# Experts of a pair interleaved over the partitions, one gate transfer a pair, and the routing bias moved to VectorE

## The reference

```
xn = layernorm(x)
# scan, per batch, feature d and state n of 16
dt = clamp(softplus(xn @ Wdt.T + bdt));  dA = exp(clamp(dt * A));  h = dA * h + dt * B * xn
y  = sum_n h * C + Dp * xn               # h is rescaled where its norm passes 20
# experts: 64 of them, hidden width 64, 8 chosen per token out of 4 of 8 groups
scores = sigmoid(xn @ router.T);  sfc = scores + correction_bias
groups: sum of the 2 best sfc of each group of 8, best 4 groups kept
chosen: best 8 of the kept sfc;  c = 2.5 * scores / sum(scores) for the chosen, else 0
routed = sum_e c_e * (relu(xn @ up_e)^2 @ down_e);  shared = relu(xn @ sup)^2 @ sdown
out = x + y + routed + shared
```

## Time and profile before

| | us |
|---|---|
| median of 3 runs | 610.81 |
| the runs | 602.62, 610.81, 615.13 |
| the profiled execution | 602.45 |
| its span, from the first to the last instruction | 600.7 |
| DVE (VectorE) busy in it | 498.6 |
| PE (TensorE) busy in it | 518.7 |

### The profile page before, as it was taken

One profiled execution on the slowest core, in us unless ns is written; L12 is line 12 of the kernel. 1 busy time (PEld: TensorE's weight loads), 2 busy tenths in 40 slices (PEclk: granted clock), 3 DMA queues, 4 the chain that ended last, 5 costly groups with the idle time before them and its releaser, 6 DMA issues. The chain is left out here.

```text
span 600.7 us, 8042 instructions
## 1 busy us (share of the span) xinstructions
PE 518.7 (86%) x1666; PEld 279.2 (46%) x1666; DVE 498.6 (83%) x1158; ACT 469.5 (78%) x922; POOL 468.8 (78%) x430
## 2 busy tenths in 40 slices
PE   2169889989899889998898988999899988998895
PEld 1036345545455444564454535555355544553442
DVE  3658898879988799887988799889999889886774
ACT  2758898778887798796986988888988887885662
POOL 2499798777989689786989879897899769765554
PEclk9999999997999999998999999999999999999999
DMA  9969998999999998999999999899999999899991
GB/s 203 301 176 254 257 242 232 224 249 259 251 265 260 251 279 258 244 243 251 241 279 262 272 286 254 251 268 288 272 283 244 251 263 262 237 236 243 256 250 48
DMA packets 67634, 149.34 MB, mean 249 GB/s; under 512 B 16032, under 2 KB 33024, under 8 KB 67584
## 3 DMA queue, kind: packets, MB, share of 16 engines
q1 hardware_dynamic: 65712, 147.07, 96.6%
q10 hardware_dynamic: 1872, 1.75, 1.1%
HBM read 143.03 MB, written 5.77 MB: 248 GB/s over the span
## 5 line engine op out<-in xcount | busy, mean ns | idle before, releaser
L1083 PE MATMUL DN<-act,down 128*128 128x512 f32 x512 | 264.4, 599 | 1.4 <-ACT act L710 1.3
L532 POOL TENSOR_TENSOR bc_rows<-dtx_all,bc_rows 128x512 f32<-128x512 f32 x128 | 164.1, 1283 | 87.0 <-DMA bc_rows<-bc_dram 86.8
L710 ACT ACTIVATE act<-relu 128x512 f32<-128x512 f32 x272 | 169.3, 623 | 69.7 <-DVE relu L880 63.9
L880 DVE SCALAR_TENSOR_TENSOR relu<-U,gate_rows 128x512 f32<-128x512 f32 x256 | 173.5, 678 | 42.7 <-DMA gate_rows<-gate_dram 19.2
L1033 PE MATMUL U<-x_hi,up_hi 128*128 128x512 f32 x256 | 159.0, 621 | 42.5 <-DVE relu L880 41.0
L541 POOL TENSOR_TENSOR yacc<-yacc,bc_rows 128x512 f32<-128x512 f32 x120 | 154.1, 1284 | 7.4 <-DVE bc_rows L892 7.1
L939 DVE TENSOR_TENSOR_SCAN DC<-DC,carry,bc_rows 128x512 f32<-128x512 f32 x96 | 122.7, 1278 | 0.0
L1033 PEld LDWEIGHTS U<-x_hi,up_hi 128*128 128x128 f32 x256 | 48.5, 189 | 144.7 <-DVE relu L880 105.6
L1083 PEld LDWEIGHTS DN<-act,down 128*128 128x128 f32 x512 | 96.3, 190 | 28.4 <-ACT act L710 5.6
L1035 PE MATMUL U<-x_hi,up_lo 128*128 128x512 f32 x256 | 102.0, 399 | 0.0
L1034 PE MATMUL U<-x_lo,up_hi 128*128 128x512 f32 x256 | 101.9, 398 | 0.0
(11 more groups left out here) (113 smaller groups left out, 503.8 us busy)
## 6 DMA issues: line engine op xcount, KB each, us to landing
bc_rows<-bc_dram SPq DMA_DIRECT2D x128, 512.0 KB, 10.7
gate_rows<-gate_dram SPq DMA_DIRECT2D x256, 256.0 KB, 8.7
xs<-in_L_attn_x SPq DMA_DIRECT2D x8, 256.0 KB, 5.7
down<-in_L_ffn_down_w SPq DMA_DIRECT2D x4, 512.0 KB, 7.3
xr<-in_L_attn_x SPq DMA_DIRECT2D x8, 256.0 KB, 11.5
rest_kept_dram<-rest SPq DMA_DIRECT2D x8, 256.0 KB, 9.1
out<-res SPq DMA_DIRECT2D x8, 256.0 KB, 7.7
dtx_all<-in_L_ffn_up_w SPq DMA_DIRECT2D x3, 512.0 KB, 6.6
```

What stands on the lines that cost most here:

```text
L532: g.tensor_tensor(b, dtx_all[:, sl(c)], b, ALU.mult).then_inc(dbp_done, 1)
L710: a.activation(act_at(c, slot), relu[:, slot % 2, :], ACT.Square).then_inc(sq_done, 1)
L880: v.scalar_tensor_tensor(out=relu[:, slot % 2, :], in0=U[slot % 2][:, :], scalar=0.0, in1=gate_rows[:, k // 2 % SBUFS, slot % 2, :], op0=A ...
L1083: mm(DN[:, :], w, act_at(c, slot), start=slot == 0, stop=slot == SLOTS - 1).then_inc(down_done, 1)
```

## The change

Three things change. First, the hidden units of a pair's two experts alternate over the partitions: unit i of the first expert lies on partition 2i, of the second on 2i + 1. The up weights are permuted when they are split into high and low part (read with a stride of 64 elements, in pairs), down is loaded by two DMAs a quarter, each to every second partition, and the gates of two pairs come in one transfer of 512 KB to 128 partitions, in which neighbouring partitions read from two different rows of DRAM. VectorE waits for one transfer instead of two. Second, the bias is added to the scores by VectorE, in slot 11.5, and not by GpSimd in slot 12; the wait of VectorE on GpSimd between them is gone, and so are two semaphores. Third, the routing behind it moves one slot up: VectorE's part from the group maxima to the sum of weights (slots 13 to 22.5 become 12 to 21.5), and GpSimd's L452 (slot 17 to 16) and L456, L459 (slot 18 to 17). ScalarE's slots, the later GpSimd steps and TensorE's transposes stay.

```diff
+        def side_by_side(t):
+            return t.rearrange("p (j e i) -> p j i e", e=2, i=I)
+        def paired(t):
+            return t.rearrange("p (j i e) -> p j i e", e=2, i=I)
...
-                sp.dma_start(down[:, e0 // 2:e1 // 2, :],
-                             down_in[e0:e1].rearrange("(j e) i h -> (e i) j h", e=2)).then_inc(w_down[q], 16)
+                for e in range(2):
+                    sp.dma_start(down[e:P:2, e0 // 2:e1 // 2, :],
+                                 down_in[e0:e1].rearrange("(j e) i h -> e i j h", e=2)[e]).then_inc(w_down[q], 16)
...
-                for half in range(2):
-                    for r in range(GCOPIES):
-                        part = slice(half * I + r * I // GCOPIES, half * I + (r + 1) * I // GCOPIES)
-                        row = half * PAIRS + 2 * i
-                        sp.dma_start(gate_rows[part, j, :, :],
-                                     gate_rows_of(c)[r:r + 1, row:row + 2].broadcast_to([I // GCOPIES, 2, CT])
-                                     ).then_inc(g_loaded[j], 16)
+                both = gate_rows_of(c)[0].rearrange("(e s) t -> e s t", e=2)[:, 2 * i:2 * i + 2, :]
+                sp.dma_start(gate_rows[:, j, :, :], both.unsqueeze(0).broadcast_to([I, 2, 2, CT])
+                             ).then_inc(g_loaded[j], 16)
...
-                if slot == 17:
+                if slot == 16:
                     pool.wait_ge(zpos_ready, pc + 1)
                     pool.wait_ge(log_done, pc + 1)
                     g.tensor_tensor(poly[:, :], poly[:, :], zpos[:, :], ALU.add).then_inc(sp_ready, 1)
-                if slot == 18:
+                if slot == 17:
                     pool.wait_ge(groups_ready, pc + 1)
...
-                if slot == 12:
-                    pool.wait_ge(sig_ready, pc + 1)
-                    alone(pool)
-                    g.tensor_tensor(sfc[:, :, :], sig[:, :, :], cbias[:, :].unsqueeze(1).broadcast_to([P, KB, E]),
-                                    ALU.add).then_inc(sfc_ready, 1)
...
-                g.tensor_tensor(up_lo[:, cols], up_raw[q], up_hi[:, cols].bitcast(F32),
+                g.tensor_tensor(paired(up_lo[:, cols]), side_by_side(up_raw[q]), paired(up_hi[:, cols].bitcast(F32)),
                                 ALU.subtract).then_inc(up_split, 1)
...
-                if slot == 12:
+                if slot == 25:
                     pool.wait_ge(w_late, 5 * 16)
...
-                a.activation(up_hi[:, cols], up_raw[q], ACT.Copy).then_inc(up_high, 1)
+                a.activation(paired(up_hi[:, cols]), side_by_side(up_raw[q]), ACT.Copy).then_inc(up_high, 1)
...
+                if slot == 11.5:
+                    if pc == 0:
+                        dve.wait_ge(w_late, 5 * 16)
+                    op(v.tensor_tensor, sfc[:, :, :], sig[:, :, :], cbias[:, :].unsqueeze(1).broadcast_to([P, KB, E]), ALU.add)
-                if slot in (13, 13.5, 14, 14.5):
-                    k = int(2 * (slot - 13))
+                if slot in (12, 12.5, 13, 13.5):
+                    k = int(2 * (slot - 12))
                     if k == 0:
-                        dve.wait_ge(sfc_ready, pc + 1)
+                        ch.wait(True)
...
-                if slot == 17.5:
+                if slot == 16.5:
                     ch.wait()
                     v.tensor_tensor(g1c[:, :], g1a[:, :], g1b[:, :], ALU.not_equal).then_inc(groups_ready, 1)
-                if slot in (19.5, 20):
-                    if slot == 19.5:
+                if slot in (18.5, 19):
+                    if slot == 18.5:
                         dve.wait_ge(masked_ready, pc + 1)
...
-                    dve.wait_ge(g_loaded[k // 2 % SBUFS], 32 * (k // 2 // SBUFS + 1))
+                    dve.wait_ge(g_loaded[k // 2 % SBUFS], 16 * (k // 2 // SBUFS + 1))
```

More of the change, by code:

```diff
@@ L201, in layer_program @@
         log_done = sem("log_done")
-        sig_one, sig_ready, sfc_ready = sem("sig_one"), sem("sig_ready"), sem("sfc_ready")
+        sig_one = sem("sig_one")
         cc_ready, ct_done, gate_ready, gate_stored = sem("cc_ready"), sem("ct_done"), sem("gate_ready"), sem("gate_stored")
@@ L256, in layer_program @@
         LEAD = 2
-        DVE_PREP = 11
+        DVE_PREP = 13
         POOL_PREP = 6
@@ L783, in constants @@
                     split = slice(0, E * I // QUARTERS)
-                    v.tensor_tensor(up_lo[:, split], up_raw[0], up_hi[:, split].bitcast(F32),
+                    v.tensor_tensor(paired(up_lo[:, split]), side_by_side(up_raw[0]), paired(up_hi[:, split].bitcast(F32)),
                                     ALU.subtract).then_inc(up_split, 1)
@@ L819, in prep @@
                     if k == KB - 1:
-                        i.then_inc(sig_ready, 1)
-                if slot in (13, 13.5, 14, 14.5):
-                    k = int(2 * (slot - 13))
+                        ch.then(i)
+                if slot == 11.5:
[4 more added lines that the diff above has]
+                    k = int(2 * (slot - 12))
                     if k == 0:
-                        dve.wait_ge(sfc_ready, pc + 1)
+                        ch.wait(True)
                     for q in range(k * G, (k + 1) * G):
@@ L828, in prep @@
                         ch.then(i)
-                if slot == 15.5:
+                if slot == 14.5:
                     op(v.tensor_tensor, g1a[:, :], g8[:, :, 0], g8[:, :, 1], ALU.add)
-                if slot == 16:
+                if slot == 15:
                     ch.wait(True)
@@ L835, in prep @@
                     ch.then(i)
-                if slot == 16.5:
+                if slot == 15.5:
                     op(v.memset, gtop[:, :, TOPG:], 3.0e38)
-                if slot == 17:
+                if slot == 16:
                     ch.wait(True)
@@ L844, in prep @@
                     ch.then(i)
-                if slot == 17.5:
+                if slot == 16.5:
                     ch.wait()
                     v.tensor_tensor(g1c[:, :], g1a[:, :], g1b[:, :], ALU.not_equal).then_inc(groups_ready, 1)
-                if slot in (19.5, 20):
-                    if slot == 19.5:
+                if slot in (18.5, 19):
+                    if slot == 18.5:
                         dve.wait_ge(masked_ready, pc + 1)
                         alone(dve)
-                    for k in range(KB // 2) if slot == 19.5 else range(KB // 2, KB):
+                    for k in range(KB // 2) if slot == 18.5 else range(KB // 2, KB):
                         i = v.max(top8[:, k, :], masked[:, k, :])
                     ch.then(i)
-                if slot in (20.5, 21):
+                if slot in (19.5, 20):
                     ch.wait(True)
-                    for k in range(KB // 2) if slot == 20.5 else range(KB // 2, KB):
+                    for k in range(KB // 2) if slot == 19.5 else range(KB // 2, KB):
                         i = v.match_replace(out=picked[:, k, :], in_to_replace=top8[:, k, :],
@@ L860, in prep @@
                     ch.then(i)
-                if slot == 21.5:
+                if slot == 20.5:
                     ch.wait()
@@ L864, in prep @@
                                     ALU.not_equal).then_inc(picked_ready, 1)
-                if slot == 22:
+                if slot == 21:
                     dve.wait_ge(picked_ready, pc + 1)
                     ch.then(v.tensor_tensor(masked[:, :, :], picked[:, :, :], sig[:, :, :], ALU.mult))
-                if slot == 22.5:
+                if slot == 21.5:
                     ch.wait()
@@ L1110, in chunk @@
                         if first and pair >= 3 and (pair - 3) % (PAIRS // QUARTERS) == 0:
-                            pe.wait_ge(w_down[(pair - 3) // (PAIRS // QUARTERS)], 16)
+                            pe.wait_ge(w_down[(pair - 3) // (PAIRS // QUARTERS)], 32)
                         down_mm(c, slot - 3)
```

## The result

| | us |
|---|---|
| kernel before, median of 4 runs beside it | 610.26 (602.62 to 615.13) |
| changed kernel, median of 4 runs | 583.32 (582.46 to 584.77) |
| ratio of the runs, 95% interval | 0.9692 (0.9639 to 0.9745) |

The change is faster by 3.1%. The forecast was 580, with 562 to 597 as its range.

A forecast was written before the change was run, and what follows sets the result against it. SP's DMA queue was taken to bound chunk 7 directly and chunks 0 to 6 through GpSimd's lag. 35.1, 68.6, 409.1, 54.9 and 10.1 gave 577.8; with 1.75 outside the span 579.6 us, said as 580, range 562 to 597.

The forecast's parts named there:

- Gates in one transfer: All chunks: one gate transfer takes 1.28 us instead of 2.27 a pair, so DMA ceases to bound.
- a merger without effect: Gate transfers: one whole transfer still takes 2.27 us, chunk 7 stays, about 600 us in all; chance 0.07.
- a slower mixed source: Gate transfers: switching between two DRAM rows makes one take 2.98 us, near 693 us in all; chance 0.04.
- Chunk 7: Last chunk, no longer bound by DMA: 34 slots at 1.571 us plus 1.5, 54.9 instead of 68.92 us.
- the allowance of 1.5: Chunk 7's first slots: 1.5 us added because they carry the end of chunk 6 (norms, a copy).
- Strided splits and the bias on VectorE, in chunk 0: Chunk 0: splits of up delay VectorE 0.5 us, the addition costs 0.8, the bias wait goes (2.3).
- The bias in chunks 1 to 6: Chunks 1 to 6: VectorE loses its bias wait, 0.4 us in chunk 5, and gains an addition of 0.8.
- The routing a slot sooner: Chunks 0 to 6: new VectorE waits on ScalarE's square and GpSimd's mask, together 1.3 us a chunk.
- One of its signs: Profile afterwards: chunks 1 to 6 alike within 1 us, at 66 to 69 us.
- The rival with nothing new to wait for: Routing in chunks 0 to 6: square and mask come in time, 568 us or below in all; chance 0.17.

The follow-up runs named there:

- the kept slots and moved splits: Changed kernel with the routing behind the bias in its old slots and GpSimd's three splits of up on VectorE before chunk 0: 569.2 us.
- the slots kept: Changed kernel with VectorE's addition of the bias in slot 11.5, but all the routing behind it in its old slots: 574.36 us.
- the logarithms earlier: Changed kernel with ScalarE's zpos, logarithms and two root steps one slot sooner too: 579.3 us.
- the old halves: Changed kernel with the gates again in two 256 KB transfers to 64 neighbouring partitions each: 613.42 us, ratio 1.015 to the kernel before.
- the alternating halves: Changed kernel with the gates in two 256 KB transfers again, each to every second partition: 584.97 us.

## Why the prediction was right, and where it was not

By its own sum, in us of the profiled executions:

| step | predicted | measured |
|---|---|---|
| to chunk 0 | 35.1 | 35.2 |
| chunk 0 | 68.6 | 74.7 |
| chunks 1 to 6 | 409.1 | 404.8 |
| chunk 7 | 54.9 | 57.0 |
| after it | 10.1 | 10.2 |
| span | 577.8 | 581.8 |

*Gates in one transfer.* Right in mechanism and size. I took 1.28 us for a transfer, the speed of the row transfers, 410 GB/s; 422 GB/s with the engines full is 1.24 us. In chunk 7, from 524 to 530 us, two transfers of each kind went at 400 GB/s, 1.31 us each; only the first gates of all, with the engines not yet full, landed up to 1.8 us apart. The queue ceased to bound, and the rivals of a merger without effect and of a slower mixed source fell.

*Chunk 7* is 2.1 us over. Eleven slots of chunk 6 at 1.571 us were the measure; from its third relu (517.81 us) to its last (570.96) the slots of chunk 7 took 1.71, with five waits on TensorE that sum to 3.8 us. The pace was taken too fast by 4.4 us over these 31 slots. The first slots, at 1.6 us each, needed hardly any of the allowance of 1.5, which hid part of the error.

*Strided splits and the bias on VectorE, in chunk 0.* This is the step that failed. I priced the splits at 0.5 us that reach VectorE, and the addition at 0.8 with 1.19 as its upper end, as if one GpSimd instruction could be ahead of it at most. The splits themselves are longer by a factor of 1.12, 0.8 us in all, in the middle of my 0 to 1.4:

```profile
L504 POOL TENSOR_TENSOR up_lo<-dtx_all,up_hi 128x1024 fp32r<-128x1024 f32 x2 | 5.3, 2648 | 0.0
```

But a GpSimd that lags has no gap, and the addition stood still for its whole run of four instructions: 5.03 us, 4.2 over my price, out of 6.1 that chunk 0 is over the forecast; the other 1.9 are not assigned to a term. Without GpSimd's splits the chunk takes 67.4 us. The two sentences of the Trainium skill that I had weighed were both off here: half as much again for a strided read (GPSIMD Engine Reference, Performance pitfalls for Q7 kernels) would be 3.5 us a split where 2.65 was measured, and a wait of one whole instruction (SBUF - State Buffer, Who interferes with whom) was one of four.

*The bias in chunks 1 to 6* cost 0.42 us, my low end and not the 0.8 that I took. It makes about half of the difference between 68.2 and the 67.5 that a chunk took. Two of its kind changed places and became 1.9 us shorter together over the eight executions, another 0.2 a chunk, as VectorE's mask of the chosen and its product came a slot sooner relative to GpSimd:

```profile
L867 DVE TENSOR_TENSOR picked<-picked,masked 128x256 f32<-128x256 f32 x8 | 7.7, 964 | 0.0
L871 DVE TENSOR_TENSOR masked<-picked,sig 128x256 f32<-128x256 f32 x8 | 3.2, 404 | 0.0
```

Before, the first took 416 ns and the second 1189.

*The routing a slot sooner.* Right, step by step. Chunk 5's timeline of the changed kernel, in the order of the earlier trace rows:

```profile
414.38 0.63 ACT L640 ACTIVATE poly<-wexp 128x512 f32<-128x512 f32 x1
...
417.13 0.62 ACT L710 ACTIVATE act<-relu 128x512 f32<-128x512 f32 x1
...
417.88 0.69 DVE L884 SCALAR_TENSOR_TENSOR relu<-U,gate_rows 128x512 f32<-128x512 f32 x1 [1.00 <-ACT act L710]
...
415.16 1.27 POOL L457 TENSOR_TENSOR poly<-poly,zpos 128x512 f32<-128x512 f32 x1 [0.80 <-ACT poly L640]
...
418.46 0.86 POOL L464 TENSOR_SCALAR masked<-masked 128x256 f32<-128x256 f32 x1 [0.20 <-POOL masked L461]
```

ScalarE's square ends at 417.75 and the relu waits 1.00 us for it (1.1 in the prediction); the mask ends at 419.32, late by 0.9 (0.8). Together they are 1.3 us more than the 0.62 that was there before.

So the total of 580 came out near 583.3 because an error of +6.1 in chunk 0 and +2.1 in chunk 7 met one of -4.3 in chunks 1 to 6. That they offset each other was luck; the sign and the main term stand on their own. What the prediction did not say is that with rows in time the bias comes in time on GpSimd too, so that two of the three changes had nothing left to gain. Its own sum for chunks 1 to 6 had it: the wait of 0.4 that goes against 0.8 and 1.3 that come. One of its signs failed as well: chunks 1 to 6 were not alike within 1 us but took 66.8 to 69.1, chunk 2 the longest. The rival with nothing new to wait for, at 568 or below, is nearly what the kept slots and moved splits gave.

## What to carry to other kernels

When one engine's wait is due to another's lag, look for what makes that one late before taking work from it: here faster transfers alone brought the wait of 16.1 us down to 4.2, and moving the instruction without them mostly renamed it. A transfer that can't reach all partitions should be spread over them rather than fill one half, with a large dimension outermost. And a step that is moved for the sake of a wait should go back once the wait is gone, for its new place has neighbours with a price of their own.

## What the runs showed that I had not expected

A VectorE addition with both operands in SBUF, of 416 ns, stood still through up to four GpSimd instructions in a row and ended 0.28 us after the last: 5.03 us in the changed kernel, 5.00 with the slots kept, 5.01 with the logarithms earlier, 4.49 with the old halves, 4.06 with the alternating halves, each time in chunk 0 behind a split. The engine that ran without gaps kept the other out; the one that waited didn't get a turn between two instructions. It isn't always so: in chunk 5 of the kernel before, L867 (at 431.65 us) took 1.37 us and ended 0.28 us after one GpSimd instruction, though by the trace GpSimd went straight on to its next. What decides who is served I have not tried. And the same 512 KB in one transfer took 1.24 us or 10.1 us, by the rates of the two stretches, with only the order of the source's dimensions changed.
